# A second gate computed beside the value product and the projection, in place of products of its own

## The reference

```
x = x + linear_attention(norm(x))         # L0: 64 wide, softmax-free, one head
x = x + moe_top2(norm(x)) + shared(norm(x))   # L0: 8 experts of 352, 2 chosen by a softmax gate; shared FFN of 704
x = x + window_attention(norm(x))         # L1: 16 heads of 16, window of 128 to either side,
                                          #     softmax((q k^T) / 16), then out @ Wp^T + bp
x = x + moe_top1(norm(x))                 # L1: logits = norm(x) @ Wg + bg, the expert of the largest logit,
                                          #     gelu(norm(x) @ W1[e]) @ W2[e], 1024 wide
```

## Time and profile before

| | |
|---|---|
| median of 3 runs | 1426.1 us (1425.23 to 1426.56) |
| the profiled execution's own time | 1431.44 us |
| its span in the trace | 1429.7 us |
| mean granted TensorE clock | 0.986 |
| instructions | 23605 |
| VectorE, ScalarE, GpSimd busy | 688.2, 470.6, 447.0 us |
| DMA | 208.54 MB |

### The profile page before, as it was taken

The page is one execution under the profiler, slowest core; times in us unless marked ns, Lnnn a source line. Parts: engine busy times, 40 slices in busy tenths (PEclk is TensorE's granted clock), DMA queues, the critical chain, the costliest instruction groups (busy, mean ns, idle before and its releaser), DMA issues.

```text
span 1429.7 us, 23605 instructions
## 1 busy us (share of the span) xinstructions
PE 1360.3 (95%) x7605; PEld 1010.3 (71%) x7605; DVE 688.2 (48%) x2480; ACT 470.6 (33%) x947; POOL 447.0 (31%) x533
## 2 busy tenths in 40 slices
PE   6699999999999999999999999999998999999998
PEld 4366555677777777655676767666666798999998
DVE  4455446333333333436878888878786222310000
ACT  2121211121221121123667666575656412111111
POOL 2110000153222222241554454454323333333442
PEclk9899999999999999999999999999998999999999
DMA  9800100011211212143554554544441678999996
GB/s 313 287 30 30 45 0 1 19 60 60 66 60 60 67 60 60 49 118 93 145 158 133 152 157 136 153 135 147 140 136 46 256 267 311 316 329 352 339 329 221
DMA packets 89462, 208.54 MB, mean 146 GB/s; under 512 B 11229, under 2 KB 45151, under 8 KB 79360
## 3 DMA queue, kind: packets, MB, share of 16 engines
q1 hardware_dynamic: 73664, 172.19, 36.8%
q0 software_dynamic: 12096, 32.13, 7.4%
q10 hardware_dynamic: 3584, 2.71, 0.6%
HBM read 155.74 MB, written 52.17 MB: 145 GB/s over the span
## 4 chain that ended last, share of the span: by engine, by line
PE 83%; DVE 5%; issue 4%; SPq 3%; DMA 2%; ACT 2%; POOL 1%; DVEq 0%; POOLq 0%; ACTq 0%
PE psum L795 12%; PE psum L962 10%; PE psum L972 10%; PE psum L662 8%; PE psum L774 6%; PE psum L673 6%; PE psum L821 5%; PE psum L868 5%; PE psum L843 4%; PE psum L892 3%; PE psum L922 2%; PE psum L901 2%; PE psum L753 2%; PE psum L783 2%; DVE work L1824 2%
## 5 line engine op out<-in xcount | busy, mean ns | idle before, releaser
L1824 DVE CUSTOM_DVE_ANT_0 work<-psum,mask 128x384 bf16<-128x384 f32 (+1 forms) x512 | 230.8, 485 | 73.0 <-PE psum L821 71.0
L795 PE MATMUL psum<-arena,work 128*128 x568 | 184.9, 468 | 0.4 <-issue 0.4
L821 PE MATMUL psum<-kz,qT 96*128 96x384 f32 (+1 forms) x512 | 171.6, 403 | 13.9 <-DVE small L1824 12.6
L1901 POOL DMA_INDIRECT work<-normed,token_of x71 | 67.5, 951 | 334.2 <-PE psum L753 205.7
L962 PEld LDWEIGHTS psum<-arena 128*128 128x128 f32 x1248 | 145.3, 192 | 2.2 <-issue 0.4
L962 PE MATMUL psum<-arena 128*128 128x128 f32 x1248 | 146.1, 275 | 0.0
L662 PE MATMUL psum<-arena 128*128 128x512 f32 x320 | 146.0, 594 | 0.0
L972 PE MATMUL psum<-arena 128*128 128x256 f32 x624 | 142.5, 382 | 0.8 <-issue 0.8
L1203 ACT ACTIVATE arena<-psum 128x384 f32<-128x384 f32 x256 | 112.3, 493 | 91.8 <-PE psum L843 90.7
L795 PEld LDWEIGHTS psum<-arena,work 128*128 128x128 f32 x568 | 102.1, 189 | 50.8 <-issue 1.8
L821 PEld LDWEIGHTS psum<-kz,qT 96*128 96x128 f32 x512 | 90.4, 195 | 66.9 <-DVE small L1824 40.7
(11 more groups left out here) (231 smaller groups left out, 2013.1 us busy)
## 6 DMA issues: line engine op xcount, KB each, us to landing
arena<-in_w SPq DMA_DIRECT2D x78, 1024.0 KB
strips<-hi SPq DMA_DIRECT2D x64, 256.0 KB
kz<-strips SPq DMA_DIRECT2D x64, 192.0 KB, 3.1
qT<-strips SPq DMA_DIRECT2D x32, 384.0 KB, 4.7
results<-work SPq DMA_DIRECT2D x71, 128.0 KB, 1.8
strips<-lo SPq DMA_DIRECT2D x32, 256.0 KB
normed<-work SPq DMA_DIRECT2D x14, 512.0 KB, 3.4
X<-in_x SPq DMA_DIRECT2D x8, 512.0 KB, 9.5
```

What stands on the lines that cost most here:

```text
L795: m = e.matmul(psum[:, pair[u], 0:INTER], xsT0[:, b % 2, c * P:(c + 1) * P], wu0[:, bass.ds(x, 1), c, u * INTER:(u + 1) * INTER], start=(c ...
L821: m = e.matmul(psum[:, bk, at:at + w], qT[0:ROWS_S, slot, half, i * P:(i + 1) * P], kz[slot][0:ROWS_S, hd, lo_key:hi_key], start=True, sto ...
L1824: e.tensor_tensor_reduce(masked[:, n % 2, 0:w], psum[:, bank_of["scores", u, i, hd], at:at + w], mask[:, P - off:P - off + w], 1.0, MASKED ...
L1901: e.indirect_dma_start(out=xs[:, b % 3, :], out_offset=None, in_=normed[l][0:n, :], in_offset=bass.IndirectOffsetOnAxis(ap=token_of[:, l, ...
```

## The change

The gate's weights, centred, become eight more columns of the value weights and of the projection's weights. With c = centred `Wg` and std the deviation of the second norm's input, x @ c for x after the attention is std * (norm2(x) @ c) + out @ (Wp^T c) + bp @ c. The first term comes out of the value product's bank, where VectorE scales it by std, adds bp @ c and writes it to `X[:, i, E:XW]`; the second comes with the projection and is added with the residual. The pick multiplies the sum by the third norm's rstd and adds `bg`. `Wp^T c` and `bp @ c` are made once, in the mixing phase. The projection of a tile has 264 columns, so that each tile takes a bank of its own, and the second half batch moves from step 35 to step 33.

```diff
-KVG, WA = 2 * D0 + 8, 3 * D0 + 8
+KVG, QA, WA = 2 * D0 + 8, 3 * D0 + 8, 3 * D0 + 16
-TURN_AT = (-11, 43)
+TURN_AT = -11
 def residual_due(step):
-    return spread(step, (29, 35))
+    return spread(step, (29, 33))
...
+        w_p = sb("w_p", [P, EC, XW])
+        std = sb("std", [P, NT])
+        bp_gate = sb("bp_gate", [P, NX])
...
-        w_qkv = carve(arena, 30720, EC, 3 * E)
-        w_p = carve(arena, 30720 + 1536, EC, E)
+        w_qkv = carve(arena, 30720, EC, 3 * E + NX)
...
-                b, half = k
-                return proj_added, 2 * b + half + 1
+                b, half, t = k
+                return proj_added, TPB * b + 2 * half + t + 1
...
-        def pe_gate(e, b, src, ring):
-            e.wait_ge(xnT_act, TURNED[3, b] + 1)
-            e.wait_ge(xnT_dve, TURNED[3, b] + 1)
-            bk = next_of(ring)
-            fill(e, ("gate", b), bk)
-            for t in range(TPB):
-                for c in range(EC):
-                    m = e.matmul(psum[:, bk, t * NX:(t + 1) * NX], src[:, c, t * P:(t + 1) * P], w_gate[:, c, :],
-                                 start=(c == 0), stop=(c == EC - 1))
-            m.then_inc(bank_full[bk], 1)
...
-            e.wait_ge(wa_loaded, 16 * 4)
+            e.wait_ge(wa_loaded, 16 * 3)
...
+        def pe_gate_proj(e, ring):
+            bk = next_of(ring)
+            fill(e, ("gate_proj",), bk)
+            e.wait_ge(wb_loaded, 16 * 2)
+            e.wait_ge(bp_spread, 1)
+            for n in range(EC + 1):
+                for k in range(EC):
+                    held = wp_raw[:, k, n * P:(n + 1) * P] if n < EC else bp_wide[:, k, :]
+                    m = e.matmul(psum[:, bk, n * NX:(n + 1) * NX], held, w_c[:, k, QA:WA], start=(k == 0), stop=(k == EC - 1))
+            m.then_inc(bank_full[bk], 1)
...
 (pe_mix)
+                if s == LEAD + 1:
+                    pe_gate_proj(e, ring)
...
 (pe_v)
-                m = e.matmul(psum[:, bk, 0:E], xnT[:, xs, k, t * P:(t + 1) * P], w_qkv[:, k, 2 * E:3 * E],
+                m = e.matmul(psum[:, bk, 0:XW], xnT[:, xs, k, t * P:(t + 1) * P], w_qkv[:, k, 2 * E:3 * E + NX],
...
 (pe_residual)
             if t == 0:
-                fill(e, ("residual", b, half), next_of(ring))
                 e.wait_ge(oT2_act, b + 1)
                 e.wait_ge(oT2_dve, b + 1)
-            bk = bank_of["residual", b, half]
+            bk = next_of(ring)
+            fill(e, ("residual", b, half, t), bk)
             at = (2 * half + t) * P
             for c in range(EC):
-                m = e.matmul(psum[:, bk, t * E:(t + 1) * E], oT2[:, c, at:at + P], w_p[:, c, :],
-                             start=(c == 0), stop=(c == EC - 1))
-            if t == 1:
-                m.then_inc(bank_full[bk], 1)
+                m = e.matmul(psum[:, bk, 0:XW], oT2[:, c, at:at + P], w_p[:, c, :], start=(c == 0), stop=(c == EC - 1))
+            m.then_inc(bank_full[bk], 1)
...
 (pe_attention; act_attention and dve_attention lose the copies in the same way)
-                    for norm, first in ((2, TURN_AT[0]), (3, TURN_AT[1])):
-                        for b, _ in batch(s, first):
-                            pe_turn_batch(e, norm, b, ring, (half,))
+                    for b, _ in batch(s, TURN_AT):
+                        pe_turn_batch(e, 2, b, ring, (half,))
...
-                            if s == GATE_AT[b]:
-                                pe_gate(e, b, xnT[:, TURNED[3, b] % 2, :, :], ring)
...
 (act_mix)
-            e.dma_start(w_gate[:, :, :], a["gate1"].rearrange("(c p) n -> p c n", p=P)).then_inc(wa_loaded, 16)
+            e.dma_start(wp_raw, a["wp"].rearrange("(c p) n -> p c n", p=P)).then_inc(wb_loaded, 16)
+            e.dma_start(bp_raw, a["bpT"]).then_inc(wb_loaded, 16)
...
 (VectorE, mixing: dve_spread_bias at step LEAD, dve_gate_proj at LEAD + 1)
+            for c in range(EC):
+                m = e.tensor_scalar(bp_wide[:, c, :], ones[:, :], bp_raw[:, c:c + 1], None, ALU.mult)
...
+            e.tensor_copy(w_gate[:, :, :], w_c[:, :, QA:WA])
+            e.wait_ge(*done["gate_proj",])
+            got = psum[:, bank_of["gate_proj",], 0:(EC + 1) * NX].rearrange("p (n x) -> p n x", x=NX)
+            e.tensor_copy(bp_gate[:, :], got[:, EC, :])
+            e.tensor_copy(w_p[:, :, E:XW], got[:, 0:EC, :]).then_inc(wp_made, 1)
...
 (dve_no_tokens)
+            e.tensor_copy(w_qkv[:, :, 3 * E:3 * E + NX], w_gate[:, :, :]).then_inc(v_gate_made, 1)
...
 (dve_pick)
-            e.wait_ge(*done["gate", b])
-            e.tensor_tensor(sc1, psum[:, bank_of["gate", b], 0:TPB * NX].rearrange("p (t x) -> p t x", x=NX),
-                            each(b_gate[:, :]), ALU.add).then_inc(scored, 1)
+            ts = slice(b * TPB, (b + 1) * TPB)
+            e.wait_ge(rstd_made, NORM[3, b] + 1)
+            yield from dve_link(e, e.tensor_tensor(sc1, X[:, ts, E:XW], wide(rstd[:, ts]), ALU.mult))
+            e.tensor_tensor(sc1, sc1, each(b_gate[:, :]), ALU.add).then_inc(scored, 1)
...
 (dve_v)
+                e.wait_ge(std_made, b + 1)
...
+            i = b * TPB + t
+            e.scalar_tensor_tensor(X[:, i, E:XW], psum[:, bank_of["v", b, t], E:XW], std[:, i:i + 1], bp_gate[:, :],
+                                   ALU.mult, ALU.add)
...
 (dve_residual)
-            e.wait_ge(*done["residual", b, half])
-            rows = X[:, t0:t0 + 2, 0:E]
-            e.tensor_tensor(rows, rows, psum[:, bank_of["residual", b, half], :].rearrange("p (t c) -> p t c", t=2),
-                            ALU.add).then_inc(proj_added, 1)
+            for t in range(2):
+                i = b * TPB + 2 * half + t
+                e.wait_ge(*done["residual", b, half, t])
+                e.tensor_tensor(X[:, i, :], X[:, i, :], psum[:, bank_of["residual", b, half, t], 0:XW],
+                                ALU.add).then_inc(proj_added, 1)
...
 (pool_scale)
+                if norm == 2:
+                    e.tensor_tensor(std[:, s], veps[:, s], rstd[:, s], ALU.mult).then_inc(std_made, 1)
```

More of the change, by code:

```diff
@@ L192 @@
 NORM = norm_numbers()
-TURNED = {k: n for n, k in enumerate(k for k in NORM if k[0])}
+NORMED = {k: n for n, k in enumerate(k for k in NORM if k[0])}
+TURNED = {(norm, b): (norm - 1) * B + b for norm in (1, 2) for b in range(B)}
 def build(nc, a, out):
@@ L525, in xn_slot @@
         def xn_slot(norm, b):
-            return TURNED[norm, b] % 2
+            return NORMED[norm, b] % 2
         def norm_number(norm, b):
@@ L880, in pe_qk @@
         def pe_qk(e, b, c, i, k, ring):
[L882 removed]
+            xs = b % 2
             if k == 0:
@@ L1146, in act_attention @@
                     act_exp(e, u, j, 0)
[L1147 to L1150 removed]
+                for b, _ in batch(s, TURN_AT):
+                    xnT_free(e, b)
+                    act_turned(e, 2, b, xnT[:, b % 2, 0, :])
                 for u, _ in unit(s, VALUES_AT + 1, 1):
```

108 lines of the change are left out of this document (57 added, 51 removed).

## The result

The changed kernel takes **1407.6 us** (median of 4 runs, 1405.8 to 1411.0), the kernel before 1426.3 on the same chip: 18.8 us faster by these medians. The ratio over all runs is 0.984 (0.981 to 0.988), which is 22.5 us. Copies of the changed kernel timed beside the kernel before in the experiments gave 0.986 (0.983 to 0.989) twice, 20 us. The forecast was 12.3 us. So the direction was right and the gain is larger by 6 to 10 us. The median of 1407.6 lies in the forecast's range of 1404 to 1422; the ratio, taken of 1426.1, gives 1403.6, just under it.

The account below looks back on a forecast made before the run. Loads bound the first 66 us, TensorE the scores (VectorE close behind) and the stretch from 1200 us. Terms -20.7 + 1.6 + 0.7 + 6.0 - 1.9 + 2.0 = -12.3 us gave 1413.8 us from 1426.1, range 1404 to 1422.

Parts of the forecast that it names:

- Banks and the moved projection: Projection's second half at step 33: 0.6 us head-output transpose wait plus 0.4 second-tile wait, six score-stage batches, +6.0 us (0 to 9).
- the gate's bank: Ahead of the maxima on TensorE: the waits for a gate's bank go, -1.9 us.
- The gate products: Eight products removed from TensorE at 1.71 us each, the half-clock sixth counted alike: 13.7 us saved.
- The tail: The stretch behind the attention scores, forecast to get 6.5 us shorter.
- The transposes: The third norm's transposes removed from TensorE, 0.87 us for each of eight batches: 7.0 us saved.
- VectorE's surplus: Net 0.6 us more VectorE work a batch, 3.6 over six batches around the scores, partly hidden: +2.0 us (0 to 3.6).
- The start: Loads up to about 65 us: 262 KB more on full DMA engines, +0.7 us (0 to 1.5).
- the columns: Value product and projection on TensorE grow from 256 to 264 columns in 256 passes: +1.6 us.
- A: Rival: VectorE truly bounds the scores stage, so only pieces behind the scores count; 1420.3 us, chance 0.17.
- B: Rival: the new waits vanish because TensorE would have waited for a mask anyway; 1405.8 us, chance 0.17.
- C: Rival: at step 34 VectorE's work makes TensorE lose 3.5 us in each of six batches; 1430.4 us, chance 0.06.
- D: Rival: thinner TensorE work meets five more half-clock stretches, giving back 10 us; 1423.6 us, chance 0.05.

Follow-up runs that it names:

- after: The changed kernel, with the whole change made to the kernel before it; 1407.6 us, median of 4 runs.
- before: The kernel without the change, on the same chip as the changed one; 1426.3 us.

## Why the prediction was right, and where it was wrong

The mechanism was right in the main: work taken from TensorE behind 650 us is worth about its own time. The sum was short by 6 to 10 us, and two of its terms failed.

**Banks and the moved projection** is the larger one. The step was "1.0 us for each of six batches within the scores: +6.0 us", with the move behind the scores at nothing. Of the waits, the head-output transpose's was sized rightly (0.47 us, six times, 2.8 in sum) and the second tile's 0.4 did not appear. But a wait was counted by itself, and what the earlier place gives was left out. Undoing the move in `after` shortens the scores by about 2 us, not by 6, lengthens the piece from the last score product to the first `pe_up1` by 3.7 us (18.9 against 15.2), and leaves the kernel 1.9 us slower. In `before` the same move shortens that piece by 4.7 us (21.3 against 16.6). The forecast held the rows for this, the idle time from 1100 to 1104 us and the half-clock stretch behind it, but only as a rival's price. Measured by whole kernels, the +6.0 should have been between about -4 and 0. The gain for the gate's bank (-1.9) is there: the maxima no longer wait for it. The first projection tile waits longer for `qT` (7.2 us against 5.0) and no longer for a list piece (2.5), so its waits are no loss.

**The gate products.** The step was "Eight of them are 13.7 us", and with it "That half-clock stretch will land on other work, so I count 1.71 for it too". At full clock one costs 1.71 us, as said. Put back into `after` they cost 16.7 us: 10.2 for the work, less than 13.7 because they partly stand where TensorE would have waited, and 6.6 for the clock that falls behind them. That 6.6 belongs to the kernel with the moved half. In `before` as it was, the profile has no half-clock stretch between 700 and 1050 us and its copy has one, of less than 4 us; with the moved half it has three, and `after` with the products put back has four, in both runs. Padding them in `before` gained between 0.8 and 4.0 us. So of the 18.8 to 22.5 us of the change the clock behind the gate products holds a few us at most. And the stretch in rows 4 and 5 did not need the sixth gate product: with that product in place and the projection moved it is gone, and with the product gone and the projection at 35 it is there.

**The tail**, where the forecast had 6.5 us, gained 15.9 in the profiled pair and 11.9 between copies alike in their stall. About 4 us of this surplus are the move's; the rest is within what the experiments leave open.

**The transposes** at 7.0 us came out at 7.0 to 8.6, uncertain by 6.

**VectorE's surplus** was set at +2.0, of it 0.17 for each small fused operation; that took 0.22. Leaving the small operations out gave 4 us at most. The size stands, roughly.

**The start**: +0.7 was forecast for the loads. The store of the normed rows landed at 65.8 us (54.00 + 11.76) against 64.8: +1.0. The first score product is 1.8 us earlier than before in the profiled pair, but 0.7 later between the two copies (648.3 and 647.6), so the start gave nothing that these profiles can tell.

**The collision** of GpSimd's bias addition with VectorE's small operation was in no term: 8.6 us of waits, and 4 to 6.5 us of time when the addition is moved away. It worked against the change, so without it the forecast would have been short by as much more.

Taken together: gate products -10.2 for the work and 0 to -4 for the clock, transposes -7.0 to -8.6, the moved half 0 to -4, against +1.6 for the columns and +1.0 for the loads (neither tested alone) and 1 to 4 for VectorE. That spans about -11 to -23 us around the measured -19 to -22.5. The sum agrees with the measurement, but it is too wide to test a single term.

**The rivals.** A (VectorE is the bound) is refuted: the scores stage is shorter by 7.9 us in the profiled pair and 5.2 between the copies, with VectorE's share at 85% of it (373.5 of 439.2). The Trainium skill, "Perfetto Trace Analysis", section "Identifying the Most-Contended Engine", says that matmul busy time is not a good measure of how close TensorE is to its limit, and names the share of weight loads beside a count of the arithmetic done. By the weight loads TensorE stood at 67% of the stage (299.57 of 447.00) and VectorE at 82%, which is rival A and 1420.3 us. The time speaks against ranking the two engines so here. B's time, 20.3 us under `before`, was met, and its reason was not: it had the new waits vanish, and 2.8 us of them are there. That it fits is luck; other terms made up for them, the move behind the scores above all. C (slower, from 2.8 us a batch at step 34): the wait there is 0.47. D (the clock; by its own working 1413.8 + 10 = 1423.8, not 1423.6) did not come: the mean clock of the scores is 0.98 as before, and between 700 and 1050 us `after` has no half-clock stretch.

## What to carry to other kernels

Read the granted clock of the microseconds behind a chain of matmuls with few columns before you count on its duration: in the changed kernel eight such chains cost 10.2 us for themselves and 6.6 in what followed them, and padding took the second part away. In the kernel before padding gained 4.0 us at most, so try it and measure. When work is taken out or moved, look at what lies beside it on the other engines: here a 2.4 us GpSimd operation came to stand on a small VectorE operation and cost 4 to 6.5 us, and moving it by two steps or cutting it in four gave them back. Price a moved step at its old place as well as at its new one, and in every stage that it touches: this one costs about 2 us among the scores, the collision included, and saves about 4 behind them. And when the kernel you compare with has two kinds of executions, look at the list of times before you believe a ratio of 0.3%.

## What the runs showed of the hardware

A fall of the granted clock came with no idle TensorE. In a copy of `before` it stood at 0.50 from 819 to 822 us, right behind a gate product whose successor started at 818.58, with TensorE busy 3.00 of 3.00 us there and 3.59 of 4.00 from 814 to 818:

```profile
814.00:818.00 4.00, 3.59 (x25) 2.93 (x24) 3.96 (x20) 3.12 (x7) 3.06 (x5) 1.00 0.38 131
819.00:822.00 3.00, 3.00 (x12) 2.64 (x11) 0.81 (x5) 0.60 (x1) 0.00 (x0) 0.50 0.49 162
```

In the profiled `before` the gate product of 876.84 has like surroundings and no fall behind it:

```profile
874.00:878.00 4.00, 3.58 (x26) 2.96 (x24) 3.97 (x20) 3.12 (x7) 3.08 (x5) 1.00 0.35 127
879.00:882.00 3.00, 3.00 (x27) 2.33 (x29) 2.15 (x9) 1.89 (x4) 0.63 (x1) 1.00 0.48 162
```

So a fall is possible behind such a product and not forced; what decides between the two is open. Between 700 and 1050 us the clock fell in four of the five profiles that have 8-column gate products there (not in the profiled `before`), and in none of the thirteen that have none or have them 128 columns wide. Outside that stretch it falls in all of them, behind other work.

A 16-column VectorE operation took 1.71 us instead of 0.18 while GpSimd worked on other tiles, and ended with GpSimd's operation. The Trainium skill, "SBUF — State Buffer", section "Who interferes with whom", says that the second port pair is an exclusive lock between VectorE and GpSimd and that the one that comes second fully blocks. By that section this holds for some VectorE instructions only; a `tensor_scalar` from SBUF to SBUF, as this one is, can be of them. The trace agrees: 1.71 us against 0.18, and 0.70 at most once the long addition stood elsewhere, while a mask that reads PSUM started inside the same addition, at 879.61, and took its usual 0.42.
